# Windowed attention on one core: value products summed four at a time, by GpSimd and by accumulating DMAs

## The chip, the cores and the metric

The kernel runs on one core of a Trainium2 chip. The metric is the device time of one launch in microseconds (us). A measurement of this kernel can tell about 0.5% (8.3 us) from no change.

## The reference, cut to what matters

The program is four layers of an attention and a feed-forward part each, on x of shape (16, 64, 512). The change touches the first attention alone. There the 64 rows of the second axis are channels (8 heads of 8 channels), the 512 positions are time, and each position looks at a window of 16 neighbours.

```python
q = _pointwise(Wq, bq, x)
k = _pointwise(Wk, bk, cond)
v = _pointwise(Wv, bv, cond)
...
k_win = k[:, :, idx].reshape(B, H, hd, T, W)
v_win = v[:, :, idx].reshape(B, H, hd, T, W)
qh = q.reshape(B, H, hd, T)
dots = jnp.einsum('bhdt,bhdtw->bhtw', qh, k_win) * scale
attn = jax.nn.softmax(dots, axis=-1)
out = jnp.einsum('bhtw,bhdtw->bhdt', attn, v_win)
out = out.reshape(B, C, T)
return _pointwise(Wo, bo, out)
...
x = x + _L0_xattn_ref(_layernorm(x, axis=-1), ctx_4096, ...)
```

So `Wo` is applied to a sum of 16 products `attn[.., w] * v[.., t + w]`. The sum may be made before `Wo`, after it, or partly before and partly after.

## The kernel before, in words

x lies in eight tiles t of 128 x 512 float32, two batches of 64 channels in each. `attn0` (L292) is the first stage; it computes projections, scores and softmax, and then comes its last part, from 119.9 to 240 us of the profile, which the change rewrites. All engines work through orders written out by hand and meet at semaphores.

- **Wide step.** The tiles go in four pairs (`PAIRS`, p), each with 16 window places w: 64 steps n = 16 p + w. In step n TensorE spreads the 8 attention rows of a batch over its 64 channels (L399): a high and a low part for two tiles, four matmuls with 32 rows each, into one of two buffers of two PSUM banks. TensorE may begin step n when the product of step n - 2 is done (`av_done`).
- **Value product.** VectorE multiplies the two banks by the shifted values (L483), 128 x 1024 numbers, into a ring of `SLOTS` = 8 buffers in the tile `window` (L297), and signals `av_done`.
- **Pair sum.** GpSimd adds two neighbouring products (L509), 32 times, and signals `pair_done`.
- **Output product.** `to_out(k)` (L382) multiplies pair sum k by `Wo` for both tiles, two float32 matmuls through `mm` (L264; in the trace each shows as two passes), and adds it up in PSUM over the 8 pair sums of a p. It is issued after wide step 2k + 5.
- **Adding to x.** `add(p)` (L468) waits for the last output product of p, adds the result to x (L472) and takes the moments of the next norm (L234, L235); it stands in VectorE's order after step 7 of the next p. The last, `add(3)`, ends the stage: `m.end` (L536) starts the expert part, on every engine and on SyncE's DMA queue.
- GpSimd also makes the reciprocal roots of the next norm (L251) after pair sum 27 and at the end.

```python
for n in range(4 * WIN):
    ...
    s.then_inc(wide_mm.sem, 1)
    if n % 2 and n >= 5:
        to_out((n - 5) // 2)
to_out(30)
to_out(31)
```

Of the kernel before, what the change touches and what calls it, by code (L numbers as in the profile page):

```python
# [11 lines left out]
ALU = mybir.AluOpType  # L12
# [3 lines left out]
P = 128  # L16
B, S, D = 16, 64, 512
# [8 lines left out]
H0, WIN = 8, 16  # L26
# [113 lines left out]
X, XT, CT, C, CONST = 0, 4096, 8192, 12288, 16384  # L140
# [122 lines left out]
def mm(pe, dst, lhsT, rhs, k=0, n=1):  # L263
    return pe.matmul(dst, lhsT=lhsT, rhs=rhs, start=(k == 0), stop=(k == n - 1))  # L264
# [27 lines left out]
def attn0(m):  # L292
# [3 lines left out]
    K0, V0 = R, R + NT * KW  # L296
    TOP, PROD = V0 + NT * KW, CT  # L297
    DOTS = TOP + D
    ATT = DOTS + WIN * D
    AV, SLOTS, SUM = DOTS, 8, PROD + 2048  # L300
    seltr = m.buf("selt_split", CT, NT * P, F32R)
    w0_in, const_in = m.sem("w0_in", 16), m.sem("const_in", 16)
    x_in, c_in = [m.sem(f"x_in{h}", 16) for h in range(2)], [m.sem(f"c_in{h}", 16) for h in range(2)]
# [3 lines left out]
    sub_done, exp_done, sum_mm, sum_done, att_done, hi_done, low_done = (  # L307
        m.sem(n, 4) for n in ("sub", "exp0", "sum_mm", "sum_done", "att", "att_hi", "att_low"))
    selt_done, wide_mm, av_done, pair_done, out_mm = (
        m.sem(n, k) for n, k in (("selt_done", 1), ("wide_mm", 64), ("av_done", 64), ("pair_done", 32), ("out0_mm", 32)))  # L310
    add_done = m.sem("add0_done", NT)
    ON_V, ON_G = ((0, 2), (4, 6), (7,)), (1, 3, 5)
    Q_BANK = {0: 0, 2: 1, 4: 2, 6: 3, 7: 4}
# [29 lines left out]
    def tensor(pe):  # L343
        pe.wait_ge(*w0_in(16))
        for n, (what, t) in enumerate(todo):
            b = place[what, t]
            earlier = [i for i in range(n) if place[todo[i]] == b]
            if earlier:
                pe.wait_ge(*proj_out(earlier[-1] + 1))
            if what == "q":  # L350
                pe.wait_ge(*m.xn_done(t + 1))
            else:
                pe.wait_ge(*c_in[t // 4](16))
            mm(pe, bank[:, b, :], f(W0 + "qkv".index(what) * P, P),
               f((XT if what == "q" else C) + t * D, D)).then_inc(proj_mm.sem, 1)
        pe.wait_ge(*const_in(16))
        pe.wait_ge(*proj_out(24))
        at = CONST + CONST_AT["selw"][0] + P - 16
        begun = set()
        for w in range(WIN):  # L360
            if w >= 3:
                pe.wait_ge(*max_done(w - 2))
            for t in TURN:
                if t in ON_G:
                    pe.wait_ge(*prod_g(w * 3 + ON_G.index(t) + 1))
                else:
                    pe.wait_ge(*prod_v(w * 3 + [t in ts for ts in ON_V].index(True) + 1))
                sel = A[:, at - 16 * (t % 2):at - 16 * (t % 2) + 32]
                second = (w, t // 2) in begun
                begun.add((w, t // 2))  # L370
                pe.matmul(bank[t // 2 * 32:t // 2 * 32 + 32, 5 + w % 3, :], lhsT=sel, rhs=f(PROD + t * D, D),
                          start=not second, stop=second).then_inc(dots_mm.sem, 1)
        for c, cut in enumerate(cuts):
            pe.wait_ge(*exp_done(c + 1))
            for w in range(WIN):
                s = mm(pe, bank[:, c, 0:P], m.const("ident"), dots[:, w, cut], w, WIN)
            s.then_inc(sum_mm.sem, 1)
        stay_busy(m, pe, 7, 22)
        pe.wait_ge(*selt_done(1))
        pe.wait_ge(*low_done(4))  # L380

        def to_out(k):  # L382
            p = k // 8
            pe.wait_ge(*pair_done(k + 1))
            if k % 8 == 0 and p >= 2:
                pe.wait_ge(*add_done(2 * (p - 1)))
            for i in range(2):
                s = mm(pe, bank[:, 4 + p % 2 * 2 + i, :], f(W0 + 3 * P, P), f(AV + (2 * k % SLOTS * 2 + i) * D, D),
                       k % 8, 8)
            s.then_inc(out_mm.sem, 1)  # L390

        for n in range(4 * WIN):
            p, w = n // WIN, n % WIN
            if n >= 2:
                pe.wait_ge(*av_done(n - 1))
            for x, part in enumerate((hi, lo)):
                for i, t in enumerate(PAIRS[p]):
                    rows = slice(t // 2 * 32, t // 2 * 32 + 32)
                    s = pe.matmul(bank[:, n % 2 * 2 + i, :], lhsT=seltr[rows, t * P:(t + 1) * P], rhs=part[rows, w, :],  # L399
                                  start=x == 0, stop=x == 1)  # L400
            s.then_inc(wide_mm.sem, 1)
            if n % 2 and n >= 5:
                to_out((n - 5) // 2)
        to_out(30)
        to_out(31)

    def vector(v):
        def scale(t):
            if t % 4 == 0:
                v.wait_ge(*m.rstd_done(t // 4 + 1))  # L410
            v.tensor_scalar(f(XT + t * D, D), f(X + t * D, D), f(MEAN + 2 * t, 1), f(RSTD + t, 1), ALU.subtract,
                            ALU.mult).then_inc(m.xn_done.sem, 1)

        def top(w):
            v.wait_ge(*dots_out(w + 1))
            if w:
                v.wait_ge(*max_done(w))
            else:
                v.wait_ge(*pads_set(5))
            v.tensor_tensor(f(TOP, D), bank[:, 5 + w % 3, :], f(TOP, D), ALU.max).then_inc(max_done.sem, 1)  # L420

        v.wait_ge(*x_in[0](16))
        for t in range(4):
            m.moments(v, 0, t)
        v.wait_ge(*x_in[1](16))
        m.moments(v, 0, 4)
        for t in range(4):
            scale(t)
        for t in range(5, NT):
            m.moments(v, 0, t)  # L430
        for t in range(4, NT):
            scale(t)
        v.wait_ge(*pads_set(4))
        for w in range(WIN):
            for i, ts in enumerate(ON_V):
                t, n = ts[0], len(ts)
                if w == 0:
                    v.wait_ge(*proj_out(todo.index(("q", ts[-1])) + 1))
                else:
                    v.wait_ge(*dots_mm(NT * (w - 1) + TURN.index(ts[-1]) + 1))  # L440
                step = ts[-1] - t
                v.tensor_tensor(spread(f(PROD + t * D, D), n, step * D, D), bank[:, Q_BANK[t]:Q_BANK[t] + n, :],  # L442
                                spread(f(K0 + t * KW + w, D), n, step * KW, D), ALU.mult).then_inc(prod_v.sem, 1)
                if i == 1 and w:
                    top(w - 1)
        top(WIN - 1)
        v.wait_ge(*max_done(WIN))
        for cut in cuts:
            v.tensor_tensor(dots[:, :, cut], dots[:, :, cut], over_w(TOP, cut), ALU.subtract).then_inc(sub_done.sem, 1)

        def divide(c):
            v.wait_ge(*sum_mm(c + 1))
            v.reciprocal(f(SUM, D)[:, cuts[c]], bank[:, c, 0:P]).then_inc(sum_done.sem, 1)
            v.wait_ge(*sum_done(c + 1))
            v.tensor_tensor(dots[:, :, cuts[c]], dots[:, :, cuts[c]], over_w(SUM, cuts[c]), ALU.mult).then_inc(att_done.sem, 1)  # L455

        def low(c):
            v.wait_ge(*hi_done(c + 1))
            v.tensor_tensor(lo[:, :, cuts[c]], dots[:, :, cuts[c]], hi[:, :, cuts[c]].bitcast(F32),  # L459
                            ALU.subtract).then_inc(low_done.sem, 1)  # L460

        divide(0)
        for c in range(1, 4):
            divide(c)
            low(c - 1)
        low(3)

        def add(p):  # L468
            v.wait_ge(*out_mm(8 * (p + 1)))
            for i, t in enumerate(PAIRS[p]):  # L470
                x = f(X + t * D, D)
                v.scalar_tensor_tensor(x, bank[:, 4 + p % 2 * 2 + i, :], bias0[:, 3:4], x, ALU.add,  # L472
                                       ALU.add).then_inc(add_done.sem, 1)
            for i, t in enumerate(PAIRS[p]):
                v.wait_ge(*add_done(2 * p + i + 1))
                m.moments(v, 1, t)

        for n in range(4 * WIN):
            p, w = n // WIN, n % WIN
            v.wait_ge(*wide_mm(n + 1))  # L480
            if n >= SLOTS:
                v.wait_ge(*out_mm((n - SLOTS) // 2 + 1))
            v.tensor_tensor(f(AV + n % SLOTS * 2 * D, 2 * D, 2, D), bank[:, n % 2 * 2:n % 2 * 2 + 2, :],  # L483
                            spread(f(V0 + PAIRS[p][0] * KW + w, D), 2, 2 * KW, D), ALU.mult).then_inc(av_done.sem, 1)
            if w == 7 and p:
                add(p - 1)
        add(3)

    def pool(g):
# [14 lines left out]
                g.tensor_tensor(f(PROD + t * D, D), f(XT + t * D, D), f(K0 + t * KW + w, D),  # L504
                                ALU.mult).then_inc(prod_g.sem, 1)
        for k in range(2 * WIN):
            at = AV + 2 * k % SLOTS * 2 * D
            g.wait_ge(*av_done(2 * k + 2))
            g.tensor_tensor(f(at, 2 * D), f(at, 2 * D), f(at + 2 * D, 2 * D), ALU.add).then_inc(pair_done.sem, 1)  # L509
            if k == 27:  # L510
                m.rsqrt_half(g, 1, 0)
        m.rsqrt_half(g, 1, 1)
# [1949 lines left out]
```

## Time and profile before

| | |
|---|---|
| three runs | 1656.92, 1659.25, 1666.53 us |
| median | 1659.25 us |
| the profiled execution | 1665.81 us, its span 1664.5 us |
| mean granted TensorE clock over the span | 0.984 of 2.4 GHz |
| busy: TensorE, VectorE, ScalarE, GpSimd | 96%, 61%, 28%, 34% |
| the part that the change rewrites | 119.87 to 238.62 us |

Times in the rows are in us unless marked ns, from the span's start. PE is TensorE, PEld its weight loads, DVE VectorE, ACT ScalarE, POOL GpSimd, SP SyncE. PEclk is the granted clock as a share of 2.4 GHz: 0.50 is 1.2 GHz. A chain row says what the end of the program waited for at that time; a timeline row merges neighbouring instructions of one line. "Idle before <-X" says what ended the engine's idle time.

### The profile page before, as it was taken

The numbers are of one execution on the slowest core, as the hardware profiler recorded it, in microseconds if no ns is written. First come the engines' busy times: TensorE is split into PE (matmuls) and PEld (weight loads), VectorE is DVE, ScalarE is ACT, GpSimd is POOL, SyncE is SP. The second block draws the span as 40 slices with busy tenths as digits, with TensorE's granted clock in tenths as the row PEclk, the third lists the DMA queues.
The fourth block names the chain that finished last, engine by engine and source line by source line (L and its number), as shares of the span: only waits on it lengthen the run. The fifth ranks groups of instructions, "written<-read, shape, count | busy, mean of one in ns | idle before, by whom it ended". The sixth has DMA issues, their size and how long they took to land.

```text
span 1664.5 us, 22246 instructions
## 1 busy us (share of the span) xinstructions
PE 1598.4 (96%) x9380; PEld 1153.3 (69%) x9380; DVE 1007.3 (61%) x1328; ACT 470.1 (28%) x682; POOL 570.7 (34%) x402
## 2 busy tenths in 40 slices
PE   8979989999989999999999999999999999899998
PEld 2264447888648877888887888878755466568886
DVE  5987765222562666564556556565661389787665
ACT  4140012000432324232433323342111456630010
POOL 3907643221155424232423313141141054462221
PEclk9989979999999999999999999999999999999999
DMA  3000022100200121011010110100300021500000
GB/s 129 1 1 0 1 95 108 35 17 33 101 13 1 38 88 42 24 63 39 26 38 26 64 31 34 39 1 1 150 4 8 19 54 28 195 1 13 14 13 14
DMA packets 18019, 66.55 MB, mean 40 GB/s; under 512 B 1440, under 2 KB 9760, under 8 KB 13312
## 3 DMA queue, kind: packets, MB, share of 16 engines
q1 hardware_dynamic: 17920, 65.12, 11.3%
q8 instruction: 75, 1.23, 0.3%
q14 instruction: 24, 0.20, 0.0%
HBM read 58.82 MB, written 2.10 MB: 37 GB/s over the span
## 4 chain that ended last, share of the span: by engine, by line
PE 84%; DVE 11%; issue 2%; ACT 1%; POOL 1%; DMA 1%; SPq 0%; DVEq 0%; ACTq 0%; POOLq 0%
PE banks L270 47%; PE banks L264 30%; PE banks L399 2%; DVE arena L442 2%; PE banks L1920 1%; PE banks L1324 1%; PE banks L2193 1%; DVE arena L234 1%; DVE window L483 1%; DVE window L420 1%; DMA arena<-in_x 1%; ACT dense L2054 1%; DVE window_split L459 1%; PE banks L283 1%; DVE window L455 0%
## 5 line engine op out<-in xcount | busy, mean ns | idle before, releaser
L270 PE MATMUL banks<-grouped_split 128*128 128x512 f32 x1536 | 367.8, 394 | 1.8 <-DVE grouped_split L1470 1.2
L270 PEld LDWEIGHTS banks<-grouped_split 128*128 128x128 f32 x1536 | 283.1, 188 | 66.4 <-issue 6.3
L1610 POOL TENSOR_TENSOR arena<-arena,attn_tables 128x512 f32<-128x512 f32 x80 | 102.2, 1282 | 298.9 <-ACT arena L1544 298.9
L270 PE MATMUL banks<-experts_split 128*128 128x512 f32 (+1 forms) x792 | 181.7, 392 | 1.9 <-DVE experts_split L630 1.9
L270 PEld LDWEIGHTS banks<-experts_split 128*128 128x128 f32 (+1 forms) x792 | 146.5, 185 | 36.4 <-issue 2.5
L1425 DVE TENSOR_TENSOR arena<-banks,attn_tables 128x512 f32<-128x512 f32 x80 | 54.6, 684 | 112.4 <-ACT arena L1544 111.9
L264 PE MATMUL banks<-arena 128*128 128x64 f32 (+2 forms) x698 | 109.5, 308 | 8.2 <-DMA arena<-in_c 6.4
L264 PEld LDWEIGHTS banks<-arena 128*128 128x128 f32 x698 | 95.3, 192 | 27.6 <-issue 18.5
L660 DVE SCALAR_TENSOR_TENSOR arena<-banks,experts,arena 128x512 f32<-128x512 f32 x64 | 47.6, 749 | 106.8 <-PE banks L270 106.8
L1438 DVE TENSOR_TENSOR arena<-arena 128x512 f32<-128x512 f32 x80 | 73.1, 915 | 57.2 <-POOL arena L1610 56.3
L509 POOL TENSOR_TENSOR window<-window 128x1024 f32<-128x1024 f32 x32 | 75.6, 2367 | 74.0 <-DVE window L483 73.8
L1543 ACT ACTIVATE arena<-banks 64x512 f32<-64x512 f32 x80 | 47.6, 595 | 167.2 <-PE banks L270 123.5
L264 PE MATMUL banks<-window,arena 128*128 128x128 f32 (+1 forms) x256 | 88.1, 493 | 6.5 <-ACT window L531 5.7
L483 DVE TENSOR_TENSOR window<-banks,window 128x1024 f32<-128x1024 f32 x64 | 75.2, 1219 | 29.1 <-PE banks L399 28.9
L264 PE MATMUL banks<-dense 128*32 128x64 f32 (+4 forms) x1738 | 84.1, 290 | 5.3 <-ACT dense L2054 3.4
L2423 POOL TENSOR_TENSOR dense<-dense,arena 128x512 f32<-128x512 f32 (+1 forms) x32 | 37.3, 1165 | 136.8 <-DVE dense L2300 136.8
L264 PEld LDWEIGHTS banks<-dense 128*32 128x32 f32 (+3 forms) x1738 | 55.4, 125 | 38.2 <-issue 31.0
L699 POOL TENSOR_TENSOR experts_split<-experts,experts_split 128x2048 fp32r<-128x2048 f32 x8 | 36.8, 4600 | 117.0 <-ACT experts_split L680 117.0
L1477 DVE TENSOR_TENSOR arena<-banks,arena 128x512 f32<-128x512 f32 x64 | 43.0, 680 | 53.8 <-PE banks L270 53.8
L264 PE MATMUL banks<-dense,arena 128*32 128x128 f32 (+1 forms) x640 | 74.4, 340 | 0.0
L264 PEld LDWEIGHTS banks<-window,arena 128*128 128x128 f32 x256 | 40.6, 212 | 38.4 <-issue 30.2
L2396 ACT ACTIVATE ht_hi<-banks 128x512 fp32r<-128x512 f32 (+1 forms) x32 | 17.4, 545 | 159.9 <-PE banks L2193 159.9
(289 smaller groups left out, 2974.3 us busy)
## 6 DMA issues: line engine op xcount, KB each, us to landing
grouped<-in_attn SPq DMA_DIRECT2D x16, 1024.0 KB, 5.1
experts<-in_expert SPq DMA_DIRECT2D x8, 1024.0 KB, 4.8
linear<-in_ffn SPq DMA_DIRECT2D x1, 4096.0 KB, 13.4
grouped<-in_attn SPq DMA_DIRECT2D x8, 512.0 KB, 3.6
dense<-arena SPq DMA_DIRECT2D x16, 256.0 KB, 4.7
dense<-in_w SPq DMA_DIRECT2D x1, 3584.0 KB, 12.1
dense<-in_attn SPq DMA_DIRECT2D x1, 3072.0 KB, 13.6
dense<-in_w SPq DMA_DIRECT2D x1, 2688.0 KB, 10.0
```

The source lines that it names most:

```text
L264: return pe.matmul(dst, lhsT=lhsT, rhs=rhs, start=(k == 0), stop=(k == n - 1))
L270: s = pe.matmul(dst, lhsT=lhsT[i], rhs=rhs[j], start=(k == 0 and x == 0), stop=(k == n - 1 and x == 2))
L483: v.tensor_tensor(f(AV + n % SLOTS * 2 * D, 2 * D, 2, D), bank[:, n % 2 * 2:n % 2 * 2 + 2, :], spread(f(V0 + PAIRS[p][0] * KW + w, D), 2, ...
L509: g.tensor_tensor(f(at, 2 * D), f(at, 2 * D), f(at + 2 * D, 2 * D), ALU.add).then_inc(pair_done.sem, 1)
L660: v.scalar_tensor_tensor(x, bank[:, t, :], f(WREP + e * NT + t, 1), x, ALU.mult, ALU.add).then_inc(x_done.sem, 1)
L699: g.tensor_tensor(r(EXS + e % 2 * 2 * LOT + LOT, LOT), f(STAGED + e % 3 * LOT, LOT), r(EXS + e % 2 * 2 * LOT, LOT).bitcast(F32), ALU.subtr ...
L1425: v.tensor_tensor(f(QC + i % 2 * HALF, HALF), bank[:, place(u), :], COS[:, h * HALF:(h + 1) * HALF], ALU.mult).then_inc(bank_v.sem, 1)
L1438: v.tensor_tensor(to, qc, rot, ALU.add).then_inc(rot_add.sem, 1)
L1477: v.tensor_tensor(x, bank[:, place(u), :], x, ALU.add).then_inc(bank_v.sem, 1)
L1543: act.activation(rot[0:64, :], bank[64:P, b, :], ACT.Copy)
L1610: g_.tensor_tensor(rot, rot, SIN[:, h * HALF:(h + 1) * HALF], ALU.mult).then_inc(rot_sin.sem, 1)
L2423: g.tensor_tensor(blocks, blocks, m.const("down32").unsqueeze(1).broadcast_to([P, nb, BLK]), ALU.mult).then_inc(eq_done.sem, 1)
```

## The change

- GpSimd still adds products in pairs, 32 times. After each second pair sum it waits for its own `pair_done` and issues a DMA from its queue that adds this pair sum (512 KB) onto the one before it in SBUF (`accum_op=ALU.add`). There are 16 of these; they signal one of four semaphores `four_done`, in turn.
- `to_out(q)` takes the sum of four products: 16 output products, where there were 32. It is issued after wide step 4q + 11, where pair k went after step 2k + 5; two are left for the end.
- The ring has 16 buffers: the 8 of before, and 4 each in the places of the key window (`K0`) and of the normed x (`XT`), which are no longer read by then.
- VectorE, before it writes a buffer again, waits by its place in the four: for the output product (first), for the pair sum (second and fourth), for the DMA (third).
- `add(p - 1)` moves from after step 7 to after step 11 of the next p.

```diff
-    AV, SLOTS, SUM = DOTS, 8, PROD + 2048
+    SLOTS, SUM = [DOTS + j * 2 * D for j in range(8)] + [at + j * 2 * D for at in (K0, XT) for j in range(4)], PROD + 2048
+    NS, NQ = len(SLOTS), WIN // 4
+
+    def four_done(q):
+
+        return fours[q % 4](16 * (q // 4 + 1))
...
         def to_out(k):
-            p = k // 8
-            pe.wait_ge(*pair_done(k + 1))
-            if k % 8 == 0 and p >= 2:
+            p = k // NQ
+            pe.wait_ge(*four_done(k))
+            if k % NQ == 0 and p >= 2:
                 pe.wait_ge(*add_done(2 * (p - 1)))
             for i in range(2):
-                s = mm(pe, bank[:, 4 + p % 2 * 2 + i, :], f(W0 + 3 * P, P), f(AV + (2 * k % SLOTS * 2 + i) * D, D),
-                       k % 8, 8)
+                s = mm(pe, bank[:, 4 + p % 2 * 2 + i, :], f(W0 + 3 * P, P), f(SLOTS[4 * k % NS] + i * D, D), k % NQ, NQ)
...
-            if n % 2 and n >= 5:
-                to_out((n - 5) // 2)
-        to_out(30)
-        to_out(31)
+            if n % 4 == 3 and n >= 11:
+                to_out((n - 11) // 4)
+        to_out(14)
+        to_out(15)
...
-            v.wait_ge(*out_mm(8 * (p + 1)))
+            v.wait_ge(*out_mm(NQ * (p + 1)))
...
-            if n >= SLOTS:
-                v.wait_ge(*out_mm((n - SLOTS) // 2 + 1))
-            v.tensor_tensor(f(AV + n % SLOTS * 2 * D, 2 * D, 2, D), bank[:, n % 2 * 2:n % 2 * 2 + 2, :],
+            if n >= NS:
+                old = n - NS
+                if old % 4 == 0:
+                    v.wait_ge(*out_mm(old // 4 + 1))
+                elif old % 4 == 2:
+                    v.wait_ge(*four_done(old // 4))
+                else:
+                    v.wait_ge(*pair_done(old // 2 + 1))
+            v.tensor_tensor(f(SLOTS[n % NS], 2 * D, 2, D), bank[:, n % 2 * 2:n % 2 * 2 + 2, :],
...
-            if w == 7 and p:
+            if w == 11 and p:
                 add(p - 1)
...
         for k in range(2 * WIN):
-            at = AV + 2 * k % SLOTS * 2 * D
+            to, other = (f(SLOTS[(2 * k + x) % NS], 2 * D) for x in (0, 1))
             g.wait_ge(*av_done(2 * k + 2))
-            g.tensor_tensor(f(at, 2 * D), f(at, 2 * D), f(at + 2 * D, 2 * D), ALU.add).then_inc(pair_done.sem, 1)
+            g.tensor_tensor(to, to, other, ALU.add).then_inc(pair_done.sem, 1)
+            if k % 2:
+                g.wait_ge(*pair_done(k + 1))
+                g.dma_start(f(SLOTS[(2 * k - 2) % NS], 2 * D), to, accum_op=ALU.add).then_inc(fours[k // 2 % 4].sem, 16)
```

TensorE's order at the start of this part, before: L399 is a wide step's matmuls (four to a step), L264 from `window` an output product (two matmuls).

```order
L264 MATMUL banks<-arena 128x256 x22
L399 MATMUL banks<-window_split,selt_split 128x512 x24
L264 MATMUL banks<-window,arena 128x512 x2
L399 MATMUL banks<-window_split,selt_split 128x512 x8
L264 MATMUL banks<-window,arena 128x512 x2
L399 MATMUL banks<-window_split,selt_split 128x512 x8
```

And of the changed kernel, where the wide steps are L405; every fourth output product reads its buffer in `arena` (the part at `XT`).

```order
L264 MATMUL banks<-arena 128x256 x22
L405 MATMUL banks<-window_split,selt_split 128x512 x48
L264 MATMUL banks<-window,arena 128x512 x2
L405 MATMUL banks<-window_split,selt_split 128x512 x16
L264 MATMUL banks<-window,arena 128x512 x2
L405 MATMUL banks<-window_split,selt_split 128x512 x16
```

Twelve wide steps stand ahead of the first output product, where there were six, and four between two of them, where there were two.

GpSimd's order at the same place in the changed kernel, with its waits (L521 is a pair sum, L524 the DMA); before, the pair sums followed each other with nothing between.

```order
L521 TENSOR_TENSOR window<-window 128x1024 [waits av_done] x2
L524 DMA window<-window 128x1024 [waits pair_done]
L521 TENSOR_TENSOR window<-window 128x1024 [waits av_done] x2
L524 DMA window<-window 128x1024 [waits pair_done]
L521 TENSOR_TENSOR window<-window 128x1024 [waits av_done] x2
L524 DMA window<-window 128x1024 [waits pair_done]
L521 TENSOR_TENSOR arena<-arena 128x1024 [waits av_done] x2
```

A DMA now stands behind every second pair sum, and the next pair sum behind the DMA.

## Rows read from the trace of the kernel before

**Rows 1.** The page, busy time of engines and the chain's shares by line

```profile
PE 1598.4 (96%) x9380; PEld 1153.3 (69%) x9380; DVE 1007.3 (61%) x1328; ACT 470.1 (28%) x682; POOL 570.7 (34%) x402
...
PE banks L270 47%; PE banks L264 30%; PE banks L399 2%; DVE arena L442 2%; PE banks L1920 1%; PE banks L1324 1%; PE banks L2193 1%; DVE arena L234 1%; DVE window L483 1%; DVE window L420 1%; DMA arena<-in_x 1%; ACT dense L2054 1%; DVE window_split L459 1%; PE banks L283 1%; DVE window L455 0%
```

**Rows 2.** The chain in order of time: start, us, what (one steady pair)

```profile
142.82 1.13 PE banks L399 x8
143.96 1.91 PE banks L264 x4
145.87 1.13 PE banks L399 x8
```

**Rows 3.** Timeline of the same pair: start, us, engine, [idle before <-releaser]

```profile
142.92 2.36 POOL L509 TENSOR_TENSOR window<-window 128x1024 f32<-128x1024 f32 x1 [0.68 <-DVE window L483]
143.52 2.35 DVE L483 TENSOR_TENSOR window<-banks,window 128x1024 f32<-128x1024 f32 x2 [0.68 <-PE banks L399]
```

**Rows 4.** Timeline of the first wide steps

```profile
120.86 2.36 DVE L483 TENSOR_TENSOR window<-banks,window 128x1024 f32<-128x1024 f32 x2 [1.14 <-PE banks L399]
122.14 2.35 PE L399 MATMUL banks<-window_split,selt_split 32*128 32x512 f32 x8 [0.47 <-DVE window L483]
...
123.40 2.36 DVE L483 TENSOR_TENSOR window<-banks,window 128x1024 f32<-128x1024 f32 x2 [0.18 <-PE banks L399]
124.68 2.35 PE L399 MATMUL banks<-window_split,selt_split 32*128 32x512 f32 x8 [0.19 <-DVE window L483]
```

**Rows 5.** Granted clock by stretch: us, busy of PE, PEld, DVE, ACT, POOL, PEclk, DMA

```profile
119.80:130.50 10.70, 9.97 (x28) 4.22 (x28) 7.08 (x6) 0.00 (x0) 6.83 (x3) 0.52 0.00 0
130.50:156.00 25.50, 25.50 (x105) 11.49 (x104) 19.14 (x17) 0.00 (x0) 17.72 (x9) 1.00 0.00 1
...
161.10:164.00 2.90, 1.43 (x10) 0.62 (x9) 2.90 (x3) 0.00 (x0) 0.67 (x1) 1.00 0.00 0
188.90:191.90 3.00, 1.33 (x8) 0.59 (x8) 3.00 (x4) 0.00 (x0) 0.57 (x1) 1.00 0.00 0
...
164.60:167.10 2.50, 2.50 (x4) 0.50 (x2) 0.91 (x1) 0.00 (x0) 2.50 (x2) 0.50 0.00 0
192.00:195.50 3.50, 3.50 (x6) 1.15 (x4) 1.51 (x2) 0.00 (x0) 3.50 (x2) 0.53 0.00 0
219.20:229.40 10.20, 10.20 (x20) 3.89 (x20) 4.57 (x4) 0.00 (x0) 6.41 (x3) 0.50 0.01 2
```

**Rows 6.** TensorE's timeline at the low clock

```profile
220.23 3.78 PE L264 MATMUL banks<-window,arena 128*128 128x512 f32 x4
223.94 2.07 PE L399 MATMUL banks<-window_split,selt_split 32*128 32x512 f32 x8
225.94 3.70 PE L264 MATMUL banks<-window,arena 128*128 128x512 f32 x4
```

**Rows 7.** The chain where an output product follows a pause of TensorE

```profile
164.04 3.15 PE banks L264 x4
...
192.05 3.55 PE banks L264 x4
```

**Rows 8.** Timeline of GpSimd, two pair sums back to back, and its shortest additions by line

```profile
163.33 4.66 POOL L509 TENSOR_TENSOR window<-window 128x1024 f32<-128x1024 f32 x2 [2.81 <-DVE window L483]
...
L251 POOL TENSOR_TENSOR arena<-arena x16: 1005/1023/1388, 14.9 to 1471.2; 128x4 f32<-128x4 f32 x16
```

**Rows 9.** Issue of a DMA on SyncE, and DMAs by line: KB each, us to landing

```profile
238.64 0.33 SPq L223 DMA_DIRECT2D experts<-in_gate  x1
...
grouped<-in_attn SPq DMA_DIRECT2D x16, 1024.0 KB, 5.1
...
grouped<-in_attn SPq DMA_DIRECT2D x8, 512.0 KB, 3.6
dense<-arena SPq DMA_DIRECT2D x16, 256.0 KB, 4.7
```

**Rows 10.** Timeline of the part's end

```profile
229.57 1.20 PE L399 MATMUL banks<-window_split,selt_split 32*128 32x512 f32 x8
...
232.78 2.35 POOL L509 TENSOR_TENSOR window<-window 128x1024 f32<-128x1024 f32 x1 [2.80 <-DVE window L483]
...
235.18 1.98 PE L264 MATMUL banks<-window,arena 128*128 128x512 f32 x4 [0.78 <-POOL window L509]
...
237.21 1.41 DVE L472 SCALAR_TENSOR_TENSOR arena<-banks,arena 128x512 f32<-128x512 f32 x2 [4.50 <-PE banks L264]
```

**Rows 11.** The chain around the first addition to x: start, us, what

```profile
156.85 1.22 DVE window L483
158.07 1.32 DVE arena L472 x2
159.38 0.61 DVE arena L234
160.02 0.18 DVE arena L235
160.20 0.59 DVE arena L234
161.06 0.97 issue
162.03 1.23 DVE window L483
```

More of the change, by code:

```diff
@@ L309, in attn0 @@
     selt_done, wide_mm, av_done, pair_done, out_mm = (
-        m.sem(n, k) for n, k in (("selt_done", 1), ("wide_mm", 64), ("av_done", 64), ("pair_done", 32), ("out0_mm", 32)))
+        m.sem(n, k) for n, k in (("selt_done", 1), ("wide_mm", 64), ("av_done", 64), ("pair_done", 32), ("out0_mm", 16)))
+    fours = [m.sem(f"four_done{i}") for i in range(4)]
     add_done = m.sem("add0_done", NT)
```

## The prediction

> **What bounds the kernel now.** I read the page's busy shares and its chain first, then the chain in order of time from 120 to 239 us, then the timeline and the granted clock of that part. TensorE is busy 96% of the span and its matmuls make up most of the chain [rows 1]. The part that the change rewrites is no exception: the chain alternates between two wide steps, 1.13 us, and one output product, 1.91 us, so a pair of steps takes 3.05 us with TensorE never idle [rows 2]. VectorE needs 2.35 us of a pair and GpSimd 2.36, each idle 0.68 [rows 3]. TensorE is the bound there, but not by much: 3.05 against 2.4.
>
> The second thing to see is the clock. It is at 1.2 GHz from 119.8 to 130.5 us and at 2.4 GHz for the steady 130.5 to 156 [rows 5]. After each `add` VectorE is late, TensorE runs only two wide steps in some 3 us (busy 1.43 of 2.9 us, 1.33 of 3.0), and right behind both lulls the clock is at 1.2 GHz: for 3.4 us twice and for 10.2 us the third time [rows 5]. At the low level an output product takes 3.15 to 3.78 us and not 1.91 [rows 6, 7].
>
> **The change part by part.** A "quad" is four wide steps and one output product.
>
> *Output products halved.* At 2.4 GHz TensorE's work of a quad falls from 2 x 3.05 = 6.1 us to 2 x 1.13 + 1.91 = 4.2 us [rows 2]. Now VectorE is slower than TensorE: 4 x 1.18 = 4.7 us [rows 3]. And the two don't overlap fully, because only two PSUM buffers lie between them. Written out from the end of the fourth wide step: output product 1.9, next wide step 0.57; the one after it goes at once, but the third waits for VectorE's product of the first (0.1 + 1.2 us after that step), the fourth for the second product (1.2 more), and takes 0.57 itself. From the end of the output product to the end of the fourth wide step that is 0.57 + 0.1 + 2 x 1.2 + 0.1 + 0.57 = 3.7 us. The quad takes 1.9 + 3.7 = 5.6 us.
>
> *GpSimd.* It keeps its 32 pair sums, 2 x 2.33 us per quad when back to back [rows 8], and gets 16 DMA issues and 16 waits for its own sum. No row shows a DMA issued by GpSimd. The nearest rows: a DMA issue on SyncE took 0.33 us [rows 9], and GpSimd's addition of 128 x 4 numbers, which is nearly all overhead, 1.0 us [rows 8]. A gain is excluded, since the instruction is added. I take 1.0 because it is this engine's own overhead, and 0.2 for wait and gaps: 4.66 + 1.2 = 5.9 us per quad; 5.2 with the lower end. Behind the waiting issue only the next pair sum is queued. So if TensorE were never slowed, GpSimd would set the pace at 5.9.
>
> *The DMAs.* 512 KB each. A plain one of that size took 3.6 us, one of 1024 KB 5.1, one of 256 KB from SBUF to SBUF 4.7 [rows 9]. An accumulating DMA reads both operands, so I take the row with twice the bytes, 5.1; the ends are 3.6 and 2 x 4.7 = 9.4. The DMA engines have nothing else here (DMA column of [rows 5]). The sum is wanted only after wide step 4q + 11, two quads later: at 7 us a quad some 12.9 us after the last product, of which pair sum, wait and issue take 2.4 + 0.1 + 1.0. That hides a DMA of up to 9.4 us, except the last. The Trainium skill, "DMA: Bandwidth & Descriptors", Anatomy of one DMA, gives a DMA from GpSimd's queue about 2.0 us plus its bytes by 436 GB/s, by estimate 3.2 us, and does not say what accumulation adds; with it the sum below would be 1.9 us less. No row here shows such a DMA.
>
> *VectorE's new waits* cost nothing: a buffer comes round after 16 steps, and the output product that frees it is issued before wide step 12 of these, which VectorE's product needs anyway. The DMA is behind that output product too. `add` moves to a place where TensorE starts an output product; it holds VectorE from 158.07 to 160.9, 2.9 us [rows 11], and VectorE is idle there at least 3.15 + 0.57 + 0.1 - 1.3 = 2.5 us. So at most 0.4 us each, 1.2 for three.
>
> *The clock.* This decides. In the lulls of before, TensorE did two wide steps in 3 us. In every quad of the change it does four in 3.7 us (busy 2.3), all with 32 rows, right between output products. The long stretch of wide steps alone, 122.1 to 127.0, did not bring the clock up although TensorE was busy 2.35 of each 2.54 us [rows 4, 5]; the output products that followed it did, as at 164.6 and 192.0 [rows 5]. I conclude that the wide stretch of a quad lets the clock fall, and that the output product, then at 1.2 GHz, brings it back. The quad becomes 3.4 us of output product (between 3.15 and 3.78 [rows 6, 7]) and 3.7 us of wide steps: **7.1 us**, over both 5.6 and 5.9.
>
> *The sum*, in the profiled execution. Twelve wide steps at the low clock, which cost 1.27 us each (2.54 for two, from 120.86) [rows 4], end at 134.7. Then 13 quads of 7.1: 92.3. The end, from the last wide step: VectorE 1.3, pair sum 2.4, wait and issue 1.1, DMA 5.1, last output product 1.9, addition to x 1.5: 13.3 (before: from 230.8 to 238.6, 7.8 [rows 10]). Adds 1.2. 134.7 + 92.3 + 13.3 + 1.2 = 241.5, where before it is 238.6. The rest of the program starts from there unchanged, at the low clock as before. **2.9 us longer.** In short: difference = 13 x quad - 89.4. The profiled execution, 1665.8 us (span 1664.5), lies 6.6 above the median of 1659.25; set against the median the forecast is 1662.
>
> **The rivals.**
>
> *A: the clock stays up.* Then the quad is GpSimd's 5.9 us, 13 x 5.9 - 89.4 = -12.7: 1647. For it: TensorE is never idle over 1 us in such a quad, and is busy 4.2 of 5.9 us. Against it: at 161.1 to 164.0 it was busy half the time and never idle over 1.1 us, and the clock fell. The Trainium skill, "TensorE: Matmul & The Clock Gate", Part 1, ties the fall to an idle stretch and the rise to sustained activity; by the letter of that rule no quad would be slowed, which is this rival and its 1647. The trace does not agree: partly busy stretches were enough for a fall. The case decides when fewer than 0.3 of the quads are slowed (a mean quad of 6.2). 0.2.
>
> *B: the clock stays down.* Mechanism: at 1.2 GHz the wide steps of a quad take longer too, so the output product, which brings the clock back, is a smaller share. From [rows 6]: output product 3.7, two wide steps 2.0, then two that wait for VectorE, 2 x 1.3: 8.35 us a quad, the output product 44% of it, where it was 3.7 of 5.7, 65%, in the low stretches of before, which nevertheless lasted 10.2 us once. Adds are then hidden, which takes off 1.2: 13 x 8.35 - 90.6 = +18: 1677. It counts as slower by over 0.5% from a quad of 7.5 on, that is when over one quad in three is low throughout. 0.25.
>
> *C: the DMA side is slow.* If a DMA takes over 9.4 us, or several can't overlap, TensorE waits at `to_out`. Three quads then take product, pair sum, wait and issue (4.8), the DMA, and one quad of 7.1; with a DMA of 12 us a quad is 23.9 / 3 = 8.0: +15; 1674. For it: the 256 KB row is slow for its size. Against: nothing else uses the queues. 0.08.
>
> *D: the change doesn't do what it says.* The output products are halved in the order of instructions, so that is not open; that this part's end doesn't move the program's is excluded by the chain, which passes through it. No chance of its own.
>
> **How the numbers follow.** The forecast (quads of 6.6 to 7.5, difference -3 to +8) gets 0.47, A 0.2, B 0.25, C 0.08. 0.5% is 8.3 us. Faster: A, with its less complete forms inside the bound, but also a fast quad with a short DMA: 0.2. Slower: B and C less their mild forms, and the forecast's upper edge: 0.33. Within: 0.47. The range takes in A at 1647 and B at 1677 with 2 us for a slow last DMA: 1647 to 1679; beyond it lie A with the short issue and C at its worst.
>
> **What would show it.** In the trace of the changed kernel: wide steps alone from 119.9 to about 134.7, clock 0.5; then output products of about 3.4 us and wide stretches of 3.7, with the clock near 0.5 in the former and 1.0 in the latter, and a quad of 7.1; GpSimd with about 1 us between its pairs and idle some 1.2 us per quad; no wait of VectorE or TensorE for a DMA but the last; landing near 5 us; the last L472 ended at about 242. A clock of 1.0 throughout with GpSimd busy end to end would be A; 0.5 throughout and 8.3 us a quad B; output products released by a DMA C. A quad under 6.6 or over 7.5 makes the forecast wrong.

## The result, and the profile after

The changed kernel takes 1677.99 us (median of 5 runs, 1677.25 to 1679.86), the kernel before 1661.1 (5 runs, 1656.92 to 1666.53). The ratio is 1.0108, 95% interval 1.0084 to 1.0132: **slower by 1.1%**; the medians lie 17 us apart. The forecast was 1662 and "no change" the likeliest; the time lies inside the range of 1647 to 1679, near its upper end.

The profiled executions differ by less, 1665.8 to 1677.9 us (spans 1664.5 and 1676.6). All of it comes from the rewritten part: its last addition to x ends at 251.2 where it was 238.6 [rows 10], 12.6 us later, and the rest of the program took 0.5 us less.

The page of the changed kernel: its summary, TensorE's clock in 40 slices, and the new DMA group.

```profile
span 1676.6 us, 22126 instructions
...
PE 1596.4 (95%) x9316; PEld 1150.5 (69%) x9316; DVE 1007.2 (60%) x1328; ACT 470.2 (28%) x682; POOL 584.9 (35%) x418
...
PEclk9986679999999999999999999999999999999999
...
window<-window POOLq DMA_DIRECT2D x12, 512.0 KB, 4.5
```

TensorE has 64 matmuls fewer and is busy 2 us less, in a span that is 12 us longer. Slices 3 to 6 (84 to 251 us) have clock 8, 6, 6 and 7 tenths; before the change the whole span had a mean of 0.984.

The same by stretch; the columns are those of [rows 5], the first two rows are the start and the steady part, the other four two output products and the wide steps behind each.

```profile
119.80:134.90 15.10, 12.87 (x48) 5.77 (x48) 13.27 (x12) 0.00 (x0) 10.55 (x5) 0.56 0.18 35
134.90:225.00 90.10, 77.82 (x226) 31.31 (x224) 58.72 (x59) 0.00 (x0) 66.22 (x36) 0.67 0.36 70
142.84:146.07 3.23, 3.23 (x8) 1.25 (x6) 1.27 (x2) 0.00 (x0) 3.18 (x2) 0.61 0.64 122
146.07:150.40 4.33, 3.08 (x18) 1.48 (x17) 3.49 (x3) 0.00 (x0) 2.59 (x3) 0.82 0.54 103
150.40:154.10 3.70, 3.70 (x7) 1.16 (x6) 1.22 (x1) 0.00 (x0) 3.51 (x2) 0.50 0.12 21
154.10:158.90 4.80, 4.33 (x18) 2.12 (x17) 3.41 (x3) 0.00 (x0) 2.02 (x2) 0.50 0.56 113
```

The kernel before, in the same stretch:

```profile
134.90:225.00 90.10, 85.49 (x310) 36.65 (x312) 69.02 (x71) 0.00 (x0) 63.77 (x28) 0.93 0.00 1
```

TensorE is now busy 78 us of the 90 and not 85, but its clock is 0.67 and not 0.93. The first of the two quads is the alternation that was forecast: output product at a low clock (3.23 us at 0.61), wide steps at a high one (0.82). But the clock falls before the wide stretch ends, and so the stretch takes 4.3 us and not 3.7. The second quad is low throughout: 3.7 + 4.8 = 8.5 us.

The timeline of that first quad shows where the 4.3 us go.

```profile
142.84 3.23 PE L264 MATMUL banks<-window,arena 128*128 128x512 f32 x4
146.00 1.19 PE L405 MATMUL banks<-window_split,selt_split 32*128 32x512 f32 x8
146.77 3.49 DVE L495 TENSOR_TENSOR window<-banks,window 128x1024 f32<-128x1024 f32 x3 [2.59 <-PE banks L405]
146.90 0.88 POOL L524 DMA_DIRECT2D arena<-arena  x1 [0.30 <-POOL arena L521]
148.05 0.73 PE L405 MATMUL banks<-window_split,selt_split 32*128 32x512 f32 x4 [0.85 <-DVE window L495]
149.18 1.22 PE L405 MATMUL banks<-window_split,selt_split 32*128 32x512 f32 x4 [0.40 <-DVE window L495]
...
150.33 3.78 PE L264 MATMUL banks<-window,arena 128*128 128x512 f32 x4
```

Two wide steps at once, then a pause of 0.85 us for VectorE's product, one at the high clock (0.73 us), a pause of 0.40, and one that takes 1.22 us: the clock has fallen again, and the next output product takes 3.78 us. GpSimd's DMA issue takes 0.88 us behind a wait of 0.30. The end of the part:

```profile
238.26 5.03 PE L264 MATMUL banks<-window,arena 128*128 128x512 f32 x8
242.31 0.88 POOL L524 DMA_DIRECT2D arena<-arena  x1 [0.30 <-POOL arena L521]
246.85 2.89 PE L264 MATMUL banks<-arena 128*128 128x512 f32 x4 [3.57 <-DMA arena<-arena]
249.78 1.41 DVE L478 SCALAR_TENSOR_TENSOR arena<-banks,arena 128x512 f32<-128x512 f32 x2 [10.19 <-PE banks L264]
```

Only here does an engine wait for a DMA, 3.6 us; it landed 4.5 us after its issue, as all 16 did (4.4 to 4.6).

### The profile page after: what moved, and what is told of

It reads as the page before. It is cut to its first block, busy times and chain, and to the rows that moved or that the text cites. A ratio compares the mean times of both kernels' runs of the same rounds, so it can differ in the third digit from the quotient of the medians.

```text
span 1676.6 us, 22126 instructions
## 1 busy us (share of the span) xinstructions
PE 1596.4 (95%) x9316; PEld 1150.5 (69%) x9316; DVE 1007.2 (60%) x1328; ACT 470.2 (28%) x682; POOL 584.9 (35%) x418
## 4 chain that ended last, share of the span: by engine, by line
PE 83%; DVE 11%; issue 3%; ACT 1%; POOL 1%; DMA 1%; SPq 0%; DVEq 0%; ACTq 0%
PE banks L270 47%; PE banks L264 31%; PE banks L405 2%; DVE arena L448 2%; PE banks L1935 1%; DVE window L495 1%; PE banks L1339 1%; PE banks L2208 1%; ACT dense L2069 1%; DVE window L426 1%; DVE window_split L465 1%; DVE arena L234 0%; DVE window L461 0%; PE banks L283 0%; DVE ht_lo L2338 0%
## 5 line engine op out<-in xcount | busy, mean ns | idle before, releaser
L264 PE MATMUL banks<-arena 128*128 128x64 f32 (+2 forms) x714 | 123.5, 325 | 11.6 <-DMA arena<-in_c 6.6
L264 PEld LDWEIGHTS banks<-arena 128*128 128x128 f32 x714 | 99.9, 195 | 37.0 <-issue 25.4
L264 PE MATMUL banks<-dense 128*32 128x64 f32 (+4 forms) x1738 | 85.0, 290 | 5.2 <-ACT dense L2069 3.5
L264 PEld LDWEIGHTS banks<-dense 128*32 128x32 f32 (+3 forms) x1738 | 55.7, 125 | 38.8 <-issue 31.5
L264 PE MATMUL banks<-dense,arena 128*32 128x128 f32 (+1 forms) x640 | 74.8, 339 | 2.7 <-issue 2.7
L521 POOL TENSOR_TENSOR window<-window 128x1024 f32<-128x1024 f32 x24 | 56.9, 2402 | 56.8 <-DVE window L495 56.7
L495 DVE TENSOR_TENSOR window<-banks,window 128x1024 f32<-128x1024 f32 x48 | 56.3, 1220 | 31.0 <-PE banks L405 30.9
L405 PE MATMUL banks<-window_split,selt_split 32*128 32x512 f32 x256 | 57.1, 557 | 17.6 <-DVE window L495 11.2
L405 PEld LDWEIGHTS banks<-window_split,selt_split 32*128 32x128 f32 x256 | 26.6, 242 | 56.7 <-DVE window L495 26.5
L264 PE MATMUL banks<-window,arena 128*128 128x128 f32 (+1 forms) x176 | 58.5, 499 | 5.7 <-ACT window L546 5.7
```

The source lines that it names most:

```text
L495: v.tensor_tensor(f(SLOTS[n % NS], 2 * D, 2, D), bank[:, n % 2 * 2:n % 2 * 2 + 2, :], spread(f(V0 + PAIRS[p][0] * KW + w, D), 2, 2 * KW, D ...
L521: g.tensor_tensor(to, to, other, ALU.add).then_inc(pair_done.sem, 1)
```

## The experiments

Two theories stood against each other. **The clock**: the order of output products and wide steps decides TensorE's clock, and the clock the time. **The added work**: the DMAs, their issue on GpSimd and the long way from product to output product bound the quads, and the low clock is only a by-product of TensorE waiting. Each kernel ran at least 6 times beside the kernel before, whose 77 runs beside them have medians of 1658.2 to 1659.3 us and lie between 1656.4 and 1670.5: 53 of them up to 1660.7, the other 24 from 1663.8 on. The profiled execution of before, 1665.8 us, is one like the 24; the profiles of two kernels below whose TensorE order in this part is that of before (experiments 2 and 9) show the more frequent kind.

**1. The DMAs left out** (`e1_no_dma`), TensorE's order kept. Half of the value products are missing from the result. TensorE, and VectorE in the same way, wait for pair sums instead.

```diff
-            pe.wait_ge(*four_done(k))
+            pe.wait_ge(*pair_done(2 * k + 2))
...
-            if k % 2:
-                g.wait_ge(*pair_done(k + 1))
-                g.dma_start(f(SLOTS[(2 * k - 2) % NS], 2 * D), to, accum_op=ALU.add).then_inc(fours[k // 2 % 4].sem, 16)
```

> The changed kernel with its 16 accumulating DMAs left out: each output product reads the first pair sum of its four alone, so half of the value products are missing from the result. TensorE's order is the changed one. Theory 1 (the clock: wide steps alone let it fall, the output product runs at 1.2 GHz): the quads stay at 7.5 to 8.5 us, mean 7.95, and only the end gets shorter by issue and landing of the last DMA, some 6 us: about 1672 us. Theory 2 (the DMAs or their issue on GpSimd cost the time): quads of 6 to 7.1 us, 1648 to 1662 us.

Measured: 1674.74 us, ratio 1.0066 (1.0044 to 1.0087). In its profile the quads and the clock are as with the DMAs:

```profile
134.90:225.00 90.10, 77.86 (x224) 31.16 (x224) 58.59 (x59) 0.00 (x0) 54.66 (x24) 0.67 0.00 0
```

TensorE's busy time and clock are those of the changed kernel to 0.04 us and 0.01. The part ends at 246.3 us, 4.9 earlier than in the changed kernel, nearly all of it behind the last wide step; the whole kernel is 3 us faster. The DMAs don't bound the quads.

**2. DMAs and ring kept, output products per pair** (`e4_pairs_and_dma`). There are 15 DMAs; they add into a buffer that nobody reads, each issued when the one before it has landed.

```diff
-            if n % 4 == 3 and n >= 11:
-                to_out((n - 11) // 4)
+            if n % 2 and n >= 5:
+                to_out((n - 5) // 2)
...
+            if k % 2 and k < 31:
+                g.wait_ge(*pair_done(k + 1))
+                if k > 1:
+                    g.wait_ge(*four_done(k // 2 - 1))
+                g.dma_start(f(CT + 2560, 2 * D), to, accum_op=ALU.add).then_inc(fours[k // 2 % 4].sem, 16)
```

> The ring of 16 buffers and 15 accumulating DMAs from GpSimd as in the changed kernel, but into a buffer that nobody reads, and TensorE's order of before: 32 output products, one per pair sum. The result is complete. Theory 1 (the clock): TensorE bounds with 6.1 us for four steps, GpSimd has 5.9, the time is that of the kernel before within 5 us: 1658 to 1666 us. Theory 2 (issue, accumulation or the contention of the DMAs costs): 1670 us or more.

Measured: 1659.07 us, ratio 0.9997 (0.9972 to 1.0022): no difference from before. With experiment 1 this places the loss: it comes with TensorE's new order and goes with it; DMAs, issue and ring cost nothing that shows while TensorE needs 6.1 us for four steps.

**3. Useless output products** (`e2_zero_products`). With zero weights, between the second and third wide step of each quad, so that TensorE works as much as before the change.

```diff
+            for i in range(2):
+                mm(pe, bank[:, 4 + p % 2 * 2 + i, :], f(ZERO, P), f(W0, D), k % NQ, NQ + 1)
...
+            if n % 4 == 1 and n >= 9:
+                to_zero((n - 9) // 4)
```

> The changed kernel plus 16 useless output products with zero weights, each between the second and third wide step of a quad, so that TensorE's work is as much as before the change. Theory 1 (the clock): the clock stays at 2.4 GHz but for the first 15 us and behind the additions to x, a quad takes 6.1 us and not 7.95, and the kernel gets faster by some 20 us although it does more work: about 1656 us. Theory 2 (a quad is bound by DMAs, GpSimd or the coupling of TensorE and VectorE): the added products cost 1.9 to 3.7 us each: 1700 us or more.

Measured: 1661.87 us, ratio 0.9999 (0.9979 to 1.0019). **More work makes the changed kernel 16 us faster.** TensorE's timeline and the stretch row of this kernel:

```profile
148.34 1.99 PE L264 MATMUL banks<-arena 128*128 128x512 f32 x4
150.25 1.20 PE L412 MATMUL banks<-window_split,selt_split 32*128 32x512 f32 x8
151.38 1.98 PE L264 MATMUL banks<-window,arena 128*128 128x512 f32 x4
...
134.90:225.00 90.10, 86.96 (x306) 37.30 (x306) 64.92 (x64) 0.00 (x0) 71.04 (x39) 0.89 0.39 76
```

The pairs are the 3.04 us of before [rows 2], and a quad 6.1 us instead of 7.95, wherever the clock is up. The profiled execution was the slowest of the 12 (1669.8 us), so 0.89 is a low value for this kernel; the median is 6 us above the 1656 expected. That settles the rival: a quad that DMAs or GpSimd bound could not get shorter by added work.

**4. The same with 32 rows** (`e8_zero_32rows`): is it the pauses or the wide steps' few rows that let the clock fall?

```diff
-                mm(pe, bank[:, 4 + p % 2 * 2 + i, :], f(ZERO, P), f(W0, D), k % NQ, NQ + 1)
+                mm(pe, bank[:, 4 + p % 2 * 2 + i, :], f(ZERO, P)[0:32, :], f(W0, D)[0:32, :], k % NQ, NQ + 1)
```

> As the kernel with 16 useless output products, but the added matmuls have 32 rows, as the wide steps have, and not 128; they have as many columns and should take as long. It tells what it is in wide steps that lets the clock fall. If time without matmuls is the cause (in a quad of the changed kernel TensorE pauses some 1.4 us of 3.7), these fill it as well: 1660 to 1664 us, clock near 1.0 from 135 us on. If it is the few rows: the clock falls as in the changed kernel and the added products only cost time at 1.2 GHz, 8.4 + 3.7 us a quad at worst: 1690 to 1730 us.

Measured: 1672.07 us, ratio 1.0091 (1.0057 to 1.0125), between the two expectations.

```profile
134.90:225.00 90.10, 83.95 (x295) 35.99 (x292) 62.17 (x62) 0.00 (x0) 67.68 (x38) 0.80 0.36 70
```

The clock is 0.80: better than the 0.67 without them, worse than the 0.89 of the same products with 128 rows. The added products took nearly as long (1.87 us, with 128 rows 1.98). In this kernel both count: matmuls with few rows held the clock less well than full ones, but better than pauses. That pauses alone are not the cause shows at 150.1 us, where the clock fell behind 9.6 us in which TensorE was busy throughout:

```profile
140.50:150.10 9.60, 9.60 (x45) 5.30 (x44) 7.48 (x7) 0.00 (x0) 7.27 (x6) 1.00 0.29 55
...
150.11 3.50 PE L264 MATMUL banks<-window,arena 128*128 128x512 f32 x4
```

**5. Output products cut in two** (`e3_split`), no work added.

```diff
-            if n % 4 == 3 and n >= 11:
-                to_out((n - 11) // 4)
-        to_out(14)
+            if n % 4 == 3 and n >= 11:
+                to_out((n - 11) // 4, (0,))
+            if n % 4 == 1 and n >= 13:
+                to_out((n - 13) // 4, (1,))
+        to_out(13, (1,))
+        to_out(14)
```

> The changed kernel with each output product cut in two: the half for one tile after the fourth wide step of a quad, the half for the other tile two wide steps later. No work is added. Theory 1 (the clock, set by how the output products lie among the wide steps): if pieces of 0.95 us every two steps hold the clock, the quad is GpSimd's 5.9 to 6.1 us and the kernel takes about 1654 us; if they don't, the clock is at 1.2 GHz throughout and a quad takes TensorE's 3.7 + 4.5 = 8.2 us, about 1681 us. Theory 2 (the clock is only a by-product, the loss is in DMAs and GpSimd): nothing changes, 1676 to 1680 us with the clock as in the changed kernel.

Measured: 1678.94 us, ratio 1.0097 (1.0068 to 1.0126): the low branch of the clock theory. The row and the timeline are the clearest of the study:

```profile
134.90:225.00 90.10, 90.10 (x224) 36.57 (x222) 58.88 (x59) 0.00 (x0) 64.95 (x36) 0.50 0.36 70
...
146.96 2.08 PE L264 MATMUL banks<-window,arena 128*128 128x512 f32 x2
148.96 2.07 PE L407 MATMUL banks<-window_split,selt_split 32*128 32x512 f32 x8
```

TensorE is busy 90.1 of 90.1 us, and the clock is at 1.2 GHz all the time. Half output products (2.0 us at this level) alternate with two wide steps (2.0), 8.0 us a quad; nothing pauses, and the clock never rises. The Trainium skill, "TensorE: Matmul & The Clock Gate", Part 1, says that sustained activity brings the full clock; this trace does not agree: half of the activity was matmuls with 32 rows, and the clock stayed down. Whole output products of 3.7 us did bring it back, here and before.

**6. Half the dose** (`e5_zero_half`): one useless half output product per quad, `to_zero` for the first tile alone.

```diff
+            if n % 4 == 1 and n >= 9:
+                to_zero((n - 9) // 4)
```

> The changed kernel with a useless half output product (zero weights, 128 rows, one tile) in the middle of each quad: half the dose. The clock theory, if half is enough: the quad goes from TensorE's 6.1 us (whole dose) to GpSimd's 5.9 to 6.0, 1 to 3 us faster than the whole dose: 1658 to 1661 us. If half isn't enough, the clock is low in part of the quads: 1665 to 1680 us.

Measured: 1673.72 us, ratio 1.0083 (1.0054 to 1.0112): half isn't enough everywhere. Away from the additions to x it is. There the quad is GpSimd's, at the price of rival A: the starts of its double sums are 5.90 us apart.

```profile
154.27 4.99 POOL L532 TENSOR_TENSOR window<-window 128x1024 f32<-128x1024 f32 x2
159.55 0.88 POOL L535 DMA_DIRECT2D window<-window  x1 [0.30 <-POOL window L532]
160.17 4.98 POOL L532 TENSOR_TENSOR window<-window 128x1024 f32<-128x1024 f32 x2
```

But behind the first two additions to x the clock fell and stayed low for some 14 us.

**7. And the last four without a DMA** (`e6_half_and_last`).

```diff
-            if k % 2:
+            if k % 2 and k < 31:
...
         to_out(15)
+        to_out(15, 1)
```

> The same, and the last four products are not added by a DMA: the last two pair sums get an output product each. The last DMA's issue and landing (5.7 us, in which every engine waits) go, one output product (1.9 us) comes: 3 to 5 us less than the kernel with the useless half product: 1654 to 1658 us if the clock holds, which would beat the kernel before. A rival that the end is hidden: no difference.

Measured: 1667.97 us, ratio 1.0047 (1.003 to 1.0065), 5.8 us under the kernel with the half products, though not the 1654 to 1658 expected, since the clock fell as in experiment 6. The wait for the last DMA was on the path. The profile (of the slowest of the 12 runs, 1674.8 us) had a surprise: the first attention ended only 1.5 us later than before, but the span was 9 us longer. Most of the other 7.5 us were lost in `ffn2`, the feed-forward part of the third layer. Its clock was at 1.2 GHz from 1202 to 1216 us, and 64 short matmuls took 12.4 us. The kernel before (second row) has the same pause of 1.1 us ahead of them and kept its clock:

```profile
1200.48 12.39 PE L264 MATMUL banks<-arena 128*128 128x64 f32 x64 [1.12 <-ACT arena L1800]
1200.74 7.36 PE L264 MATMUL banks<-arena 128*128 128x64 f32 x64 [1.12 <-ACT arena L1770]
```

**8. The lulls of the kernel before filled** (`e7_before_filled`), two useless half output products behind each `add`.

```diff
+            if p and w in (9, 10):
+                mm(pe, bank[:, 4 + p % 2 * 2, :], f(ZERO, P), f(W0, D), 1, 3)
```

> The kernel before with two useless half output products (zero weights) in each of the three lulls behind the additions to x, where its own clock falls. The clock theory: no fall at the three lulls, 1.7 us or more saved at each and about 0.6 lost: 2 to 8 us faster than before, 1652 to 1657 us, and the spread of its runs (1657 to 1670 us) gets smaller, since that spread would come from how long the clock stays low after a lull. Otherwise: 1659 to 1663 us with the same spread.

Measured: 1664.16 us, ratio 1.0019 (1.0001 to 1.0038): no gain, above both expectations. Inside the first attention the clock stayed up at all three additions, as expected, and the part ended at 231.2 us, 7.4 earlier than in the profile of before. That profile is one like the 24; in the profiles of experiments 2 and 9 the part ended at 232.3 and 232.2, so the fillers gained 1 us against these. The rest of the program took 3.7 us more than before's; `ffn2` had the same fall as in experiment 7:

```profile
1194.00:1208.00 14.00, 14.00 (x56) 11.99 (x56) 4.20 (x13) 0.63 (x1) 0.00 (x0) 0.51 0.32 135
161.00:164.00 3.00, 2.86 (x11) 1.19 (x12) 2.71 (x4) 0.00 (x0) 1.70 (x1) 1.00 0.00 0
```

(the second row is the lull of [rows 5], now busy 2.86 of 3 us.)

**9. A filler in `ffn2`**, alone (`e11_before_ffn2`) and with experiment 8 (`e9_filled_twice`).

```diff
+        stay_busy(m, pe, 6, 3)
         pe.wait_ge(*m.xt_done(24 + NT))
```

> The kernel before with three short useless matmuls in the feed-forward part of the third layer (ffn2), ahead of its wait for the transposed x, where the traces of the two last filled kernels show 13 us at 1.2 GHz (from 1194 us on) and that of the kernel before none. If part of the spread of before's runs comes from there: the slower runs (1664 to 1668 us) get rarer, median 1657 to 1659 us. Otherwise no change.

> The kernel before with the three lulls of the first attention filled and the filler in ffn2. The first attention was 7.4 us shorter with the lulls filled, and 5 to 6.6 us were lost again in ffn2, where the clock fell. With both filled the kernel keeps the gain: 1653 to 1657 us, all runs within 3 us. If the loss in ffn2 has another cause than the clock: 1664 us as with the lulls alone.

Measured: alone 1658.01 us, ratio 0.9992 (0.9973 to 1.0012), runs from 1656.8 to 1666.8: nothing, and the spread is not gone. With the lulls filled 1658.77 us, ratio 0.9991 (0.9974 to 1.0008), all 12 runs between 1658.2 and 1661.4. The clock in `ffn2` holds (no fall in the profile) and the spread is gone; against experiment 8 the filler in `ffn2` alone made the kernel 5.4 us faster. But the median is not better than that of before, and the expected 1653 to 1657 was wrong. In the profile of the kernel with the filler in `ffn2` alone, the first attention ends no later than with the lulls filled (232.2 against 232.1 us). It has two falls of 3 us behind the additions, and none behind the third, where the profile of before had 10.2 us [rows 6]:

```profile
218.20 1.98 PE L264 MATMUL banks<-window,arena 128*128 128x512 f32 x4
220.11 1.19 PE L399 MATMUL banks<-window_split,selt_split 32*128 32x512 f32 x8
```

**10. All together on the changed kernel** (`e10_best`): experiment 7, two more useless half products behind each `add`, and the filler in `ffn2`.

```diff
+            if p and w in (13, 14):
+                mm(pe, bank[:, 4 + p % 2 * 2, :], f(ZERO, P), f(W0, D), 1, 3)
```

> The changed kernel with a useless half output product in each quad, the last four products without a DMA, two more useless half products behind each addition to x, where the kernel with the half products had 13 us at 1.2 GHz, and the filler in ffn2. If the clock holds behind the additions, a quad takes 5.8 us nearly everywhere: the first attention gets some 10 us shorter than in the kernel before, 1648 to 1655 us, which would beat both kernels. If the clock still falls there: 1658 to 1668 us.

Measured: 1656.31 us, 12 runs from 1653.4 to 1658.2, ratio 0.9964 (0.9945 to 0.9983).

```profile
134.90:225.00 90.10, 85.18 (x314) 34.37 (x313) 71.10 (x73) 0.00 (x0) 79.07 (x43) 0.97 0.42 82
```

The changed kernel is beaten by 22 us; the time is just above the expected 1648 to 1655. Against the kernel before, the ratio is 0.4% and the medians are 2 us apart, less than the 0.5% that a measurement can tell. The closest comparison is with experiment 9, 12 runs at the same time: 2.5 us less than the kernel before with its lulls filled, the runs meeting only at 1658.2. So once the clock is paid for with matmuls that compute nothing, the sums in fours no longer cost time, and what they gain is 2 to 3 us at most.

## Why the prediction was wrong

The mechanism was found: the likeliest case said that the wide stretch lets the clock fall and the output product brings it back, and rival B was its stronger form. Experiments 1 to 3 and 5 show it: the loss stays without the DMAs, goes with TensorE's old order, and goes when matmuls are added. What was off was the size of one term, **the quad of 7.1 us**, and with it the side on which the result lies.

- *Twelve wide steps at the low clock, to 134.7*: right. They took 14.5 us from the first matmul (120.42 to 134.92), 14.8 forecast; they began 0.5 us later than in before, so the end is 0.2 off.
- *Output product 3.4 us and wide stretch 3.7*: wrong, the step that failed. The 13 quads took 7.5 to 8.5 us, 7.95 in the mean (134.92 to 238.26): the output product 3.5 and the wide stretch 4.4, so that nearly all of the miss is in the wide stretch, which I had put at the full clock. I had priced the fourth wide step at the full clock, 0.57 us, and it often ran at the low one, 1.22; and I had let the clock come back within every output product, where after 150.33, 197.84 and 221.87 it did not, which gave three quads of 8.5. [Rows 5] had shown both ways a low stretch can last, 3.4 and 10.2 us, and I took the short one for all. 13 x 0.85 = 11.1 us. Why the clock falls within the wide stretch in some quads and behind it in others stays open.
- *Adds 1.2*: nothing measurable. The quad with the first addition took 7.7 us, less than the mean, though its pause for VectorE was 1.09 us where it is 0.85 elsewhere.
- *The end 13.3*: 12.9. The DMA landed in 4.5 us (5.1 taken), the last output product took 2.9 (1.9 taken), since TensorE had waited for it.
- *GpSimd 5.9 us a quad, issue 1.0*: right where it could show (5.90 us in experiment 6; issue 0.88 and wait 0.30). In the changed kernel it was idle some 2 us of a quad.
- *VectorE's waits, the DMAs hidden but for the last*: right (experiments 1 and 2). The formula of the Trainium skill, "DMA: Bandwidth & Descriptors", Anatomy of one DMA, 3.2 us by estimate, came out too low for this accumulating DMA: 4.4 to 4.6 us.

The sum with these: 2.9 + 0.2 + 11.1 - 1.2 - 0.4 = 12.6 us, by which the part ends later than before. The rest of the program took 0.5 us less, and the profiled executions differ by 12.1.

- *The step from the profile to the median*: also off. I set the difference against the median of three runs and gave the profiled execution 6.6 us above it no meaning. It had two low stretches of 10.2 us, the first and the one behind the third addition [rows 5]. The profiles of experiments 2 and 9 (the filler in `ffn2` alone), whose order of output products is that of before, have spans of 1655.9 and 1655.8: the first stretch lasts 7 us, behind the third addition the clock does not fall, and the part ends 6.4 us earlier. So before's usual run has less low clock than the one I read, while the changed kernel's runs agree within 2.6 us. The profiled execution lies 4.7 us above the median of 1661.1: that is the other 5 us of the 17. Against the more frequent kind of run (medians of 1658.2 to 1659.3) the change costs 19 to 20 us.
- *Rival A* (clock stays up) was wrong, and the rule of the Trainium skill, "TensorE: Matmul & The Clock Gate", Part 1, that stands beside it did not hold here: the clock fell behind wide stretches with pauses of 0.85 and 0.40 us. *Rival B* (quads of 8.35 throughout, 1677 us) hit the number by luck: three quads of thirteen were its own, the profiled difference was 12 us and not its 18, and the usual run of before, unknown to it, made up the rest. *Rival C* is excluded by experiment 1.

Open: why a fall lasts 3.4 us in one run, 10.2 in another and does not come in a third was not tried, nor why `ffn2` loses its clock in some kernels. Of ten profiles without a filler there, two show that fall (experiments 7 and 8). A shift of the first attention does not decide it: its end came 6.3 us earlier in experiment 2 and 4.2 later in experiment 6, and both kept the clock in `ffn2`. Three short fillers prevented it (experiment 9).

## What to carry to other kernels

Before you take matmuls away from a stretch that TensorE bounds only narrowly, work out the new pattern of full matmuls, small ones and pauses, and price it once at each clock level: a third less work can take longer. Check such a loss by putting the work back as matmuls with zero weights; if the kernel gets faster and its granted clock rises, it was the clock. And if the runs of a kernel spread by more than the gain that you look for, read the clock of the profiled execution first: it may not be the usual one.

## What was unexpected of the hardware

- TensorE busy without a pause for 90 us (134.9 to 225) at 1.2 GHz, with a clock share of 0.50 (experiment 5).
- Useless matmuls of 128 rows raised the clock from 0.67 to 0.89, the same with 32 rows to 0.80 (experiments 3 and 4).
- The clock fell behind 9.6 us in which TensorE had no pause, most of it 32-row matmuls (experiment 4).
- An accumulating DMA of 512 KB within SBUF landed 4.4 to 4.6 us after its issue, 16 times of 16, and its issue held GpSimd for 0.88 us (1.08 at most).
- In two kernels that differ from before only in the first attention, 64 short matmuls in `ffn2`, 950 us later, ran at 1.2 GHz and took 12.3 to 12.4 us, not 7.4. The rest of the program took 3.7 and 7.5 us longer (experiments 8 and 7); what brings the fall is not shown.
